# Post-norm attention and gated feed-forward layer on one core: Tanh gate, host-transposed input, token-major first norm with its last step on GpSimd, and new instruction orders on all engines

## What is computed

```python
Q, K, V = heads(x @ Wq.T + bq), heads(x @ Wk.T + bk), heads(x @ Wv.T + bv)   # 16 heads of 8
s = Q @ K.T / sqrt(8) - (i - j) for j <= i, else -inf
x = layernorm(x + (softmax(s) @ V) @ Wo.T + bo)
h = silu((x @ w1.T) * s1) * ((x @ w2.T) * s2)      # 128 -> 512, ternary weights
h = gelu((h @ h1.T) * h1s)                          # 512 -> 512, exact gelu
h = gelu((h @ h2.T) * h2s)                          # 512 -> 512
out = layernorm(x + (h @ w3.T) * w3s)               # 512 -> 128
```

## Time and profile before

| | us |
|---|---|
| median of 3 runs | 1059.17 (1049.75 to 1065.03) |
| the profiled execution | 1058.79 |
| its span, first to last instruction | 1057.1 |
| PE busy in the span | 908.8 (86%) |
| DVE, ACT, POOL busy | 662.0, 601.3, 457.6 |

### The profile page before, as it was taken

One profiled execution on the slowest core, in us unless ns is written; L12 is line 12 of the kernel. 1 busy time (PEld: TensorE's weight loads), 2 busy tenths in 40 slices (PEclk: granted clock), 3 DMA queues, 4 the chain that ended last, 5 costly groups with the idle time before them and its releaser, 6 DMA issues.

```text
span 1057.1 us, 19058 instructions
## 1 busy us (share of the span) xinstructions
PE 908.8 (86%) x6242; PEld 588.5 (56%) x6242; DVE 662.0 (63%) x2985; ACT 601.3 (57%) x912; POOL 457.6 (43%) x525
## 2 busy tenths in 40 slices
PE   2388889898998989899898989899898989999776
PEld 1244556565665656566565656566565656565544
DVE  4846566666657666666667677566767667573231
ACT  4144465657475564747475565747466565746555
POOL 1020334545353534535363544535363444544344
PEclk9996599899888889989899989889899989886888
DMA  6020101010100101010010101010010101000000
GB/s 224 0 76 33 43 1 66 21 64 23 64 23 30 56 2 64 23 64 23 35 51 1 67 21 64 22 64 23 33 54 1 66 21 64 13 2 12 1 11 11
DMA packets 23187, 40.65 MB, mean 38 GB/s; under 512 B 2864, under 2 KB 4528, under 8 KB 23088
## 3 DMA queue, kind: packets, MB, share of 16 engines
q1 hardware_dynamic: 23088, 39.41, 10.2%
HBM read 7.94 MB, written 4.19 MB: 11 GB/s over the span
## 4 chain that ended last, share of the span: by engine, by line
PE 72%; DVE 14%; ACT 6%; issue 4%; POOL 2%; DMA 0%; SPq 0%; POOLq 0%; DVEq 0%; ACTq 0%
PE ps L405 18%; PE ps L411 15%; PE ps L492 11%; PE ps L474 6%; DVE ps L725 5%; PE ps L450 5%; PE ps L476 4%; PE ps L510 3%; POOL hlo L881 2%; PE ps L429 2%; DVE attn L762 2%; PE ps L518 2%; PE ps L499 2%; DVE m L725 2%; ACT pt L607 2%
## 5 line engine op out<-in xcount | busy, mean ns | idle before, releaser
L881 POOL TENSOR_TENSOR hlo<-hf,hhi 128x512 fp32r<-128x512 f32 x192 | 245.9, 1284 | 383.6 <-ACT hhi L662 248.5
L725 DVE CUSTOM_DVE_ANT_0 ps<-ps,causal 128x256 f32<-128x256 f32 (+1 forms) x1024 | 332.2, 388 | 96.7 <-PE ps L453 96.1
L862 POOL TENSOR_SCALAR_AFFINE_SELECT pt<-pt 128x512 f32<-128x512 f32 x256 | 167.6, 660 | 177.1 <-ACT pt L607 169.6
L607 ACT ACTIVATE pt<-ps 128x768 f32<-128x768 f32 x256 | 196.0, 809 | 82.5 <-PE ps L476 81.8
L656 ACT ACTIVATE hf<-ps,vec_sb 128x512 f32<-128x512 f32 x128 | 88.0, 688 | 214.9 <-PE ps L411 214.9
L405 PE MATMUL ps<-hhi,h_hi 128*128 128x512 f32 x512 | 176.8, 470 | 2.0 <-ACT hhi L662 1.5
L411 PE MATMUL ps<-hlo,h_hi 128*128 128x512 f32 x512 | 152.1, 422 | 0.7 <-POOL hlo L881 0.7
L725 DVE DVE_READ_ACCUMULATOR2_ANT m<- 128x1 f32 x1024 | 142.7, 139 | 0.0
L492 PE MATMUL ps<-pt,vst 128*32 128x256 f32 (+1 forms) x2048 | 124.5, 374 | 1.8 <-DVE raw L749 0.8
L450 PE MATMUL ps<-ks,qs 32*128 32x256 f32 x512 | 105.5, 414 | 21.0 <-DVE m L725 19.9
L411 PEld LDWEIGHTS ps<-hlo,h_hi 128*128 128x128 f32 x512 | 105.9, 207 | 27.3 <-POOL hlo L881 2.3
(11 more groups left out here) (99 smaller groups left out, 1085.6 us busy)
## 6 DMA issues: line engine op xcount, KB each, us to landing
qs<-q_hi SPq DMA_DIRECT2D x32, 256.0 KB
ks<-k_hi SPq DMA_DIRECT2D x32, 256.0 KB
x_tok<-in_x SPq DMA_DIRECT2D x16, 256.0 KB, 2.8
qs<-q_lo SPq DMA_DIRECT2D x16, 256.0 KB
ks<-k_lo SPq DMA_DIRECT2D x16, 256.0 KB
out<-o_tok SPq DMA_DIRECT2D x16, 256.0 KB, 2.0
qs<-no_max SPq DMA_DIRECT2D x16, 64.0 KB
qs<-mT_sb SPq DMA_DIRECT2D x32, 32.0 KB
```

What stands on the lines that cost most here:

```text
L607: nc.scalar.activation(pt[u][:, c:c + 2, :], ps[:, first:last + 1, 0:3 * P], ACT.Exp).then_inc(t_free.sem, 1)
L725: part = nc.vector.tensor_tensor_reduce(ps[:, bank, cols], ps[:, bank, cols], mask, 1.0, LOWEST, ALU.add, ALU.max, m32[:, it, c + e, u:u + 1])
L862: nc.gpsimd.affine_select(out=diag, in_=diag, compare_op=ALU.is_ge, fill=0.0, base=0, pattern=[[0, 2], [0, 2], [1, P]], channel_multiplier ...
L881: nc.gpsimd.tensor_tensor(h_lo[layer % 2][:, m, :], hf[:, n % 4, :], h_hi[layer % 2][:, m, :].bitcast(F32), ALU.subtract).then_inc(hlo_rea ...
```

## The change

- x comes from DRAM twice: feature-major straight into `xT` (the step `qx` is gone), and token-major into `x_tok` (`tload`), to which GpSimd adds the bias bo (`xbo`).
- `wo` is computed token-major, as 4 matmuls of 128 columns. DVE adds `x_tok` (`res1`) and makes the statistics from SBUF; the transposes `zt` 1 are gone. The last step of the first norm (`lnnorm` 1) runs on GpSimd.
- `x1hi` and `x1T` are written by ACT from PSUM, `x1lo` by DVE from PSUM and `x1hi`.
- `anorm` reads the transposed result in PSUM; the copy `rT` is gone.
- silu(z) is computed as 0.5 z (1 + tanh(z/2)): ACT Tanh, DVE one more instruction for each block (`gate`, then `gmul`). The `gu` blocks move to the half of the slot with the exponentials and one slot earlier (pair t-1), as do `qq`, `qk`, `qv`. `ghi` moves from ACT to DVE.
- `w3` is cut in two (`w3h`, `w3l`) and goes to the bank `PVB`.
- Every engine has a list of its own (`PE_ORDER`, `ACT_ORDER`, ... for a full slot, `..._FILL` for pairs 0 and 1, `..._DRAIN` for the end). The score steps stand in twos. The weight split no longer stands ahead of the first score step: ACT writes `w_hi`, GpSimd `w_lo`, in two parts within the fill; weights are loaded behind the first stacks. The flag is read at the end of the fill, whose feed-forward products use `w_lo` too.

```diff
-AFTER_S = {
-    0: [("gu", 0), ("pv", 1, 3)], 1: [("gu", 1), ("araw", 1), ("ghi", 0)], 2: [("gu", 2), ("atr", 1), ("anorm", 1), ("ghi", 1)],
...
+PE_ORDER = [
+    ("s", 0, 0, 0), ("pv", 1, 1, -1), ("pv", 1, 2, -1), ("s", 0, 1, 0), ("s", 0, 2, 0), ("pv", 1, 3, -1),
+    ("atT", 0, -1), ("h", 1, 0, -2), ("s", 0, 3, 0), ("s", 0, 4, 0), ("h", 1, 1, -2), ("s", 0, 5, 0),
...
             def load_x(q):
-                sp.dma_start(x_tok[:], x[q]).then_inc(x_loaded.sem, 16)
+                sp.dma_start(xT[q % 2][:], x[q]).then_inc(x_loaded.sem, 16)
...
                         elif kind == "wo":
...
-                            pe.matmul(ps[:, ONE, :], wo_sb[:], attT[:], start=True, stop=True
-                                      ).then_inc(l_full.sem, 1)
+                            for j in range(TT):
+                                last = pe.matmul(ps[:, ONE, j * P:(j + 1) * P], attT[:, j * P:(j + 1) * P],
+                                                 wo_sb[:], start=True, stop=True)
+                            last.then_inc(l_full.sem, 1)
...
                     elif kind == "anorm":
                         b = s[1]
-                        rT_ready.wait(dve, q, b + 1)
-                        rv = rT[:].rearrange("p a (c e k) -> p a c e k", c=C, e=2)
+                        at_full.wait(dve, q, 2 * b + 1)
+                        rv = ps[:, ONE, :].rearrange("p (a c e k) -> p a c e k", a=4, c=C, e=2)
...
+                    elif kind == "tanh":
+                        m = s[1]
+                        g_full.wait(act, q, m + 1)
+                        f_dve.wait(act, q, m - 1)
+                        nc.scalar.activation(sg[:, m % 2, :], ps[:, gate_bank(q, "g", m), :], ACT.Tanh,
+                                             scale=half_s1[:, m:m + 1]).then_inc(f_tanh.sem, 1)
...
+                    elif kind == "gate":
+                        m = s[1]
+                        f_tanh.wait(dve, q, m + 1)
+                        nc.vector.scalar_tensor_tensor(
+                            out=sg[:, m % 2, :], in0=sg[:, m % 2, :], scalar=1.0, in1=ps[:, gate_bank(q, "g", m), :],
+                            op0=ALU.add, op1=ALU.mult).then_inc(f_gate.sem, 1)
...
+                        nc.vector.tensor_copy(h0(q)[0][:, m, :], gated(q, m)).then_inc(h0hi_ready.sem, 1)
...
+                    elif s == ("lnnorm", 1):
+                        l_full.wait(pool, q - 1)
+                        carry(pool, "pool")
+                        ln_rstd[0].wait(pool, q)
+                        for j in range(TT):
+                            nc.gpsimd.tensor_scalar(
+                                x1[:, j, :], zT[0][:, j * P:(j + 1) * P], mv[0][:, j, 0:1],
+                                rstd[0][:, j:j + 1], ALU.subtract, ALU.mult).then_inc(ln_part[0].sem, 1)
```

More of the change, by code:

```diff
@@ L43 @@
 U, C = 4, 4
+HP = H // 2
 BIG = -(2.0 ** 100)
@@ L54 @@
 MAX_FIRST, MAX_STEP = 15, 16
-AFTER_S = {
-    0: [("gu", 0), ("pv", 1, 3)], 1: [("gu", 1), ("araw", 1), ("ghi", 0)], 2: [("gu", 2), ("atr", 1), ("anorm", 1), ("ghi", 1)],
-    3: [("gu", 3), ("ghi", 2)], 4: [("atT", 1), ("ghi", 3), ("table", "gelu")],
[3 rows of a table removed]
-}
-AFTER_ST = {
-    0: [("w3",)], 1: [("mT", 1), ("res2",)], 4: [("zt", 2), ("lnstat", 2)], 5: [("rstd", 2)],
-    6: [("x1t",)], 7: [("lnnorm", 2)], 8: [("xload",), ("x1split",)], 11: [("araw", 0)], 13: [("atr", 0), ("anorm", 0)],
-    15: [("atT", 0), ("table", "silu")],
-}
@@ L112 @@
[L112 to L121 removed]
+FIRST_PIECES = 5
+PE_FILL = [
[17 rows of a table added]
+]
@@ new lines, with fill_steps, slot_steps, in_one @@
+SP_DRAIN = [
+    ("store", -2), ("store", -1),
+]
+ONE_KINDS = ("qq", "qk", "qv", "mT", "atr", "atT", "wo", "zt", "x1t")
+FULL_SLOTS = range(2, PAIRS)
+LAST = PAIRS - 1
+def fill_steps(fill):
+    return [(tuple(s), q) for *s, q in fill]
+def slot_steps(order, drain):
+    full = [(tuple(s), t + d) for t in FULL_SLOTS for *s, d in order if t + d < PAIRS or s[0] == "table"]
+    return full + [(tuple(s), PAIRS + d) for *s, d in drain]
+def in_one(s, q):
+    return s[0] in ONE_KINDS
+ONE_USES = [e for e in fill_steps(PE_FILL) + slot_steps(PE_ORDER, PE_DRAIN) if in_one(*e)]
@@ L851, in _, with run @@
                 nc.gpsimd.memset(vst[i][:], 0.0).then_inc(vst_zero, 1)
-            def slot(t, par, stages, before):
-                for s, q, p in steps(t, par, stages):
-                    kind = s[0]
+            def run(steps):
+                for s, q in steps:
+                    kind, p = s[0], q % 2
                     if kind == "sel":
```

690 lines of the change are left out of this document (400 added, 290 removed), and 35 rows, old and new, of tables (AFTER_S, PE_DRAIN, PE_FILL, PE_ORDER).

## The result

The changed kernel takes 840.17 us (838.58 to 851.31, 4 runs) against 1055.06 (1049.75 to 1065.03): a ratio of 0.796 (0.789 to 0.802).

What follows compares the result with a forecast made beforehand. PE was taken as the bound, its slot being work, idling and slow clock. 49.2 + 2.7 + 1.6 gave 53.5 us a slot; fill 121, 14 slots 749, end 66 and 1.7 outside gave 938 us, range 900 to 992.

Steps and rivals of the forecast that it cites:

- PE's work, 50.2 to 49.2 us: Full slot: PE work at 2.4 GHz loses eight transposes, about 0.5 us per four; `wo` as four matmuls taken as 0.
- Idling, 5.4 to 2.7 us: Idle PE in a full slot: 5.4 less 4.3 us of long waits, plus 1.6 us for three places late next.
- The norm step: First norm's `lnnorm` on GpSimd, ahead of `x1t`: four steps taken as 1.3 us, chain 7.2 us, hidden behind PE's 8.6.
- The maxima: Row maxima on DVE in the score half: 1 us of PE idling a slot, between 0 and 4.
- Slow clock, 4.6 to 1.6 us: Full slot: PE time lost at 1.2 GHz, falling from 4.6 to 1.6 us as long waits go.
- in the proportion of the waits: Full slot: slow clock scaled by long waits followed by it, one or two instead of three or four; 1.6 us.
- Fill, 22 + 46 + 51 + 2: Before the full slots: first score step at 22 us, two slots of 46 and 51, 2 more for `w_lo`; 121 us.
- End, 66: After the full slots: 79 us less 6 (gate products), 3 (`attn` wait) and 4 (`x1` of pair 15); 63 to 70.
- rival 1: Full slots: the clock doesn't recover, 18% stays at 1.2 GHz; slot 56.5 us, 980 us; chance 0.22 with rival 2.
- rival 2: GpSimd and DVE hold each other anew, `ghi` beside `hlo`; slot 56 us, 973 us; chance 0.22 with rival 1.
- Rival 3: Full slots: DVE's foreign pieces each stop PE, slow clock following; slot 72 us, 1190 us; chance of slower 0.04.

Runs made afterwards that it cites:

- the repeat: The changed kernel measured again with nothing altered: 841.62 us, ratio 0.799 to the kernel before.
- The products from the bank: Kernel before, with ACT's copy of the turned heads removed and DVE's products reading PSUM: 974.34 us, ratio 0.924.
- before with the first stall gone: Kernel before with DVE's products reading PSUM, 974.34 us; with score steps put in twos as well, 1033.4 us, ratio 0.981.

## Why the prediction was wrong

By its own sum: fill 121, measured 110.6; slots 749, measured 666.9; end 66, measured 61.8. 82 of the 97 us are the slot, 53.5 against 47.6. The account that follows is of the slot first.

- **PE's work, 50.2 to 49.2 us: the step that failed.** The forecast took before's work less eight transposes, and a pair of score steps at 0.74 us, twice 0.37. A two takes 0.40. In a slot of the repeat with a clock of 1.00 (347.4 to 395.0) PE is busy for 45.5 us, 3.7 less than forecast, and 3.7 us is the difference that the twos make to the score steps (12.6 us a slot without them, 8.9 with them). The steps in twos had a term in the forecast for what they would cost in waits and none for what they save. The order showed thirteen twos in the slot, and that odd and even steps use different rows is in the code (`c = 2 * (n % 2) + e`). The saving could be seen in one row of before as well, the two at 612.88. Before's own seven twos don't weaken this: with them its score steps take 12.7 us a slot, as long as with none.
- **Idling, 5.4 to 2.7 us:** measured 2.3. The waits for `attn` and `k_lo` went as walked. The norm step was taken at 0.33 us and its bounds were 0.23 and 0.64; it is 0.80, and so PE waits 1.8 us a slot ahead of `x1t`, as the forecast said it would from 0.65 on. That the sum of the idling came out so near, 2.3 against 2.7, is luck. The maxima, taken at 1 us of idling, cost none that shows among the waits.
- **Slow clock, 4.6 to 1.6 us:** right in kind; between 0 in the slots at 1.00 and about 1 us on average (0.98, half of 4% of 45 us). But "in the proportion of the waits" was wrong: one wait of three, the one for `attn`, had nearly all of it (0.91 to 0.98 by its removal alone). As PE's clock doesn't fall alike behind each wait, the forecast's 1.6 us rested on a rule that the runs don't bear out.
- The version of before with that wait gone has 54.5 us a slot, and the changed one without twos 54.1. The forecast's 53.5 lies near these two; what it described was the change without its twos.
- **Fill, 22 + 46 + 51 + 2:** measured 20.2 + 42.6 + 47.8 + 0. The clock of the second slot is 0.79, not 0.60, and no stop of PE for the flag appears in the list of waits. **End, 66:** 61.8.
- **The rivals.** The clock recovered, so rival 1 fell. Of rival 2 some is there: a `ghi` copy on DVE takes up to 1057 ns and 519 in the mean, where the earlier trace rows had 412 to 427 for its form, 0.1 us each, which PE doesn't feel. Rival 3 needed DVE to stop PE at each foreign piece, which it doesn't in this order; in the order of before, twos do it (`hf`, `m`, `pt`).

What each part is worth depends on the rest. The products from the bank give 80 us in before and 16 in the changed kernel; twos give 90 in the changed kernel, 0 in before, and cost 59 in before with the first stall gone. Between the last two stand the lists per engine and all the rest of the change, the Tanh gate and the moved `gu` blocks among it. That it is the lists that turn the twos' work into time is argued from the waits; a version of before with lists per engine and nothing else wasn't run. Nor were the fill and the end, 42 of the 217.8 us of span, the transposed input and `wo` token-major taken apart.
